# Layer 0 attention as one sequence of 576 steps: value products that lag across groups, output rescaling spread over three engines

## What is computed

```python
qkv = x @ Wqkv                       # x is the normalised, modulated input
q = qkv[..., :2 * Hx].reshape(Bx, 2 * NQ, Sx, HD)      # 32 query heads of 16
k = qkv[..., 2 * Hx:2 * Hx + G].reshape(Bx, NKV, Sx, HD)  # 8 key heads
v = qkv[..., 2 * Hx + G:].reshape(Bx, NKV, Sx, HD)
...
scores = jnp.where(causal, q k^T / sqrt(HD), -inf)
aw = jax.nn.softmax(scores, axis=-1)
aw = aw.reshape(Bx, NQ, 2, Sx, Sx)
aw = aw[:, :, 0] - lam * aw[:, :, 1]
attn = einsum(aw, v) * (1.0 - LAMBDA_INIT)
```

## Time and profile before

| what | us |
|---|---|
| median of three runs (2429.91 to 2431.61) | 2430.19 |
| the profiled execution, its own time | 2430.3 |
| its span | 2428.4 |
| a group in the steady part, from one O3 to the next | 114.88 |
| start of the first step, end of the last output | 129.4, 1947 |

### The profile page before, as it was taken

How to read it: one execution, slowest core, us unless ns; L and a number is a source line. 1 busy time by engine, 2 the same in 40 slices (tenths; PEclk the granted TensorE clock), 3 DMA queues, 4 the chain that set the end, 5 groups by cost and what they waited for, 6 DMA issues and landing times. The chain is left out here.

```text
span 2428.4 us, 46606 instructions
## 1 busy us (share of the span) xinstructions
PE 2220.2 (91%) x17772; PEld 992.5 (41%) x17772; DVE 1829.4 (75%) x3782; ACT 1547.9 (64%) x3105; POOL 525.7 (22%) x584
## 2 busy tenths in 40 slices
PE   6799999999999999999999999999999979889984
PEld 4233333333333333333333333334333258567831
DVE  2788888878787888888888888887888348434467
ACT  2167677777767776767676777777767725235633
POOL 2112121303222121212121213131201014100067
PEclk8589999999999999999999999999999979899955
DMA  4120302121121202020303030212100030000001
GB/s 145 36 58 6 66 11 61 22 50 32 41 41 31 47 25 47 30 56 17 66 6 66 6 66 18 55 27 45 32 12 2 2 96 0 1 1 1 1 22 48
DMA packets 95990, 84.79 MB, mean 35 GB/s; under 512 B 48544, under 2 KB 81440, under 8 KB 95776
## 3 DMA queue, kind: packets, MB, share of 16 engines
q1 hardware_dynamic: 95776, 81.91, 15.2%
HBM read 26.81 MB, written 16.78 MB: 18 GB/s over the span
## 5 line engine op out<-in xcount | busy, mean ns | idle before, releaser
L605 DVE TENSOR_REDUCE m_part<-a_bank 128x1 f32<-128x512 f32 (+3 forms) x2560 | 1395.5, 603 | 270.0 <-PE a_bank L906 163.2
L749 ACT ACTIVATE probs<-b_bank 128x512 f32<-128x512 f32 (+1 forms) x2304 | 1173.2, 578 | 412.4 <-PE b_bank L922 407.2
L922 PE MATMUL b_bank<-q_pack,k_pack 34*128 34x512 bf16 (+7 forms) x5120 | 949.0, 348 | 6.2 <-DMA q_pack<-m_rows 1.8
L894 PE MATMUL a_bank<-k_pack,q_pack 64*128 64x512 bf16 (+3 forms) x2560 | 847.2, 357 | 58.5 <-DVE m_part L605 33.0
L960 PE MATMUL acc<-probs,v_tile 128*32 128x512 f32 (+3 forms) x5120 | 587.1, 540 | 22.6 <-ACT o_sb L756 21.5
L922 PEld LDWEIGHTS b_bank<-q_pack,k_pack 34*128 34x128 bf16 (+1 forms) x5120 | 316.5, 94 | 547.7 <-ACT probs L749 392.6
L894 PEld LDWEIGHTS a_bank<-k_pack,q_pack 64*128 64x128 bf16 x2560 | 238.2, 94 | 333.4 <-DVE m_part L605 255.2
L476 POOL TENSOR_SCALAR_AFFINE_SELECT probs<-probs 128x512 f32<-128x512 f32 (+1 forms) x192 | 151.5, 789 | 1019.4 <-ACT probs L749 1019.4
L906 PE MATMUL a_bank<-future,pick 64*128 64x128 bf16 x2048 | 278.3, 219 | 0.0
L906 PEld LDWEIGHTS a_bank<-future,pick 64*128 64x128 bf16 x2048 | 185.7, 96 | 47.5 <-issue 4.7
L960 PEld LDWEIGHTS acc<-probs,v_tile 128*32 128x32 f32 x5120 | 107.3, 108 | 186.6 <-issue 94.2
(11 more groups left out here) (193 smaller groups left out, 1761.0 us busy)
## 6 DMA issues: line engine op xcount, KB each, us to landing
q_pack<-part SPq DMA_DIRECT2D x384, 64.0 KB, 2.3
k_pack<-part SPq DMA_DIRECT2D x192, 64.0 KB, 2.3
scratch<-qkv_row SPq DMA_DIRECT2D x16, 512.0 KB, 2.8
heads<-scratch SPq DMA_DIRECT2D x16, 512.0 KB, 3.7
xg<-in_L_attn_x SPq DMA_DIRECT2D x16, 256.0 KB, 2.8
scratch<-qkv_row SPq DMA_DIRECT2D x32, 128.0 KB, 2.7
q_pack<-m_rows SPq DMA_DIRECT2D x256, 2.0 KB
x<-in_L_attn_x SPq DMA_DIRECT2D x4, 1024.0 KB, 11.7
```

Source lines behind the costliest of these rows:

```text
L605: dve.tensor_reduce(m_part[:, 2 * hp + side, t, c:c + 1], a_bank[at % A_RING][:, 0:width_a(u % UNITS)], AX.X, ALU.max).then_inc(a_maxed, 1)
L749: act.activation(probs[:, s % P_RING, h, at:C], b_bank[bank_no(("B", par, s, h))][:, at:C], ACT.Exp, scale=HD ** -0.5) \
L894: ins = pe.matmul(a_bank[at % A_RING][:, 0:w], q_pack[buf][rows, hp, 0, q:q + P], k_pack[buf][rows, 0, C * c:C * c + w], start=True, stop= ...
L922: ins = pe.matmul(b_bank[bank_no(slot)][:, at:at + C - q], k_pack[par][rows, n2, P * kt:P * (kt + 1)], q_pack[par][rows, h // 2, n2, C * j ...
```

## The change

The two nested loops over pairs of groups become one loop over `n` from 0 to 578 on every engine.

- The value products of steps 34 and 35 move from the end of their group to steps 0 and 1 of the next one. `meet_v(n - LAG)` crosses groups.
- All uses of a bank (M, O, N, W, T) move from the end of a step to its middle, behind the value product. On ACT they stand between the exponentials of heads 1 and 2. O3 comes at step 2 of the next group. M uses come one step later, T0 to T3 at 18 to 21.
- The copy of `acc` follows the first two exponentials of step `J_LAST + LAG`, and `turn_output` comes one step later.
- Rescaling: ACT copies the turned bank to `o_rows` in SBUF, DVE takes reciprocal and signs from there one step later still (the second after all maxima of that step), and POOL does the multiplication and then the pair.
- `gather_heads` goes from DVE at step 15 to POOL at step 14 for groups 2 to 15.
- The short operations on block maxima are interleaved with the maxima of the next unit; `m_part` is doubled.
- The masks of a short unit stand right behind its scores; where a unit stands alone (`score_maxima`), the two row halves alternate.
- SP issues the same DMAs in the same order with the same waits.

```diff
@@ PE
-                        if s >= LAG:
-                            meet_v(i, par, s - LAG)
-                        two_heads(i, par, s, 1, maxima(1), last)
-                        if ending:
-                            for k in range(LAG):
-                                for u in maxima(2 + k):
-                                    score_maxima(i, par, u)
-                                meet_v(i, par, s - LAG + 1 + k)
-                        for use in [u for t, u in uses_of(par, last) if t == s]:
...
+                if n < LAST_STEP and s in J_FIRST:
+                    pe.wait_ge(m_rows_in, 16 * QH * (NJ * g + J_FIRST.index(s) + 1))
...
+                if n < LAST_STEP:
+                    two_heads(n, 0, share(ahead, 0, 2))
+                if LAG <= n < LAST_STEP + LAG:
+                    meet_v(n - LAG)
+                for use in uses_at(n):
+                    wait_for_bank(use)
...
+                if n < LAST_STEP:
+                    two_heads(n, 1, share(ahead, 1, 2))
+            def score_maxima(u):
+
                 for n in range(2):
-                    unit_head(i, par, u, n)
-                    mask_head(i, par, u, n)
+                    unit_head(u, n)
+                for m in range(2):
+                    for n in range(2):
+                        mask_head(u, n, m)
@@ SP
+            for g in range(GROUPS):
+                par, more = g % 2, g + 2 < GROUPS
+                if more:
+                    load_x(g + 2, g + 2)
+                if g + 1 < GROUPS:
+                    pack(g + 1, 1 - par, STEPS * g)
+                maxima_rows(4 * g + 3, par, 2)
...
@@ ACT
+            for n in range(TAIL):
+                if n < LAST_STEP:
+                    for h in range(QH // 2):
+                        exponential(n, h)
+                if n in COPY_AT:
+                    take_output(COPY_AT[n])
+                for use in uses_at(n):
...
+                    if what == "T" and k % 4 == 3:
+                        first_part(k // 4)
+                if n < LAST_STEP:
+                    for h in range(QH // 2, QH):
+                        exponential(n, h)
+            def take_rows_of_output(block, no, bank):
+                act.wait_ge(misc_filled, no)
+                if block:
+                    act.wait_ge(o_added, block)
+                act.activation(o_rows[:, :], bank[:, :], ACT.Copy).then_inc(o_taken, 1)
@@ DVE
-                dve.reciprocal(o_rl[:, :, :], o[:, :, :, HD]).then_inc(o_step, 1)
-                dve.wait_ge(o_step, upto(2 * n + 1))
-                dve.tensor_tensor(o_w[:, :, :], o_rl[:, :, :], signs[:, :, :], ALU.mult).then_inc(o_step, 1)
...
-                dve.tensor_tensor(o_sc[:, j % 2, :].rearrange("p (t h e) -> p t h e", t=TB, h=QH), o[:, :, :, 0:HD],
+                maximum(u, 0)
+                if before is not None:
+                    negate(before)
+                maximum(u, 1)
+                if before is not None:
+                    negate_rest(before)
...
+                for k, u in enumerate(ahead):
+                    unit_maxima(u, u == UNITS * GROUPS - 1)
+                    if k == 0 and n - 1 in OUTPUT_AT:
+                        invert(OUTPUT_AT[n - 1])
...
+                if n - 1 in OUTPUT_AT:
+                    weigh(OUTPUT_AT[n - 1])
@@ POOL
+                pool.wait_ge(o_weighed, n + 1)
+                if n:
+                    pool.wait_ge(o_added, n)
+                pool.tensor_tensor(o, o_rows[:, :].rearrange("p (t h e) -> p t h e", t=TB, h=QH)[:, :, :, 0:HD],
+                                   o_w[:, :, :].unsqueeze(3).broadcast_to([P, TB, QH, HD]), ALU.mult).then_inc(o_scaled, 1)
+                pool.wait_ge(o_scaled, n + 1)
+                pool.tensor_tensor(dst, halves[:, :, :, 0, :], halves[:, :, :, 1, :], ALU.add).then_inc(o_added, 1)
```

More of the change, by code:

```diff
@@ L137 @@
-GATES_AT = 24
-SLOTS = [slot for par in range(2) for s in range(STEPS)
-         for slot in [("B", par, s, h) for h in range(QH)] + [(use, par, s, 0) for use in MISC[s]]]
-SLOTS[-1:-1] = [None] * (-len(SLOTS) % B_RING)
-def bank_no(slot):
-    return SLOTS.index(slot) % B_RING
-def occupant(slot, last):
-    at = SLOTS.index(slot) - B_RING
-    while True:
-        was = SLOTS[at % len(SLOTS)]
-        if was is not None and (at < 0 or was[0] == "B" or (was[2], was[0]) in uses_of(was[1], last)):
-            return was, at < 0
-        at -= B_RING
+LAST_STEP = STEPS * GROUPS
@@ new lines, with uses_at @@
+NEXT = [j for j in range(NJ) if A_LAST[j] < LEAD]
+PREP_AT = {7: "N", 8: "W0", 9: "W1", 10: "W2", 11: "W3", 18: "T0", 19: "T1", 20: "T2", 21: "T3"}
+COPY_AT = {STEPS * g + J_LAST[j] + LAG: 4 * g + j for g in range(GROUPS) for j in range(NJ)}
+OUTPUT_AT = {n + 1: block for n, block in COPY_AT.items()}
+MAXIMA_AT = {n + 2: 4 * (u // UNITS) + A_LAST.index(u % UNITS)
+             for n in range(LAST_STEP) for u in units(n) if u % UNITS in A_LAST}
+GATHER_AT = 14
+GATES_AT = 24
+def uses_at(n):
+    g, s = n // STEPS, n % STEPS
+    out = []
+    if n in MAXIMA_AT:
+        out.append(("M", MAXIMA_AT[n]))
+    if n in OUTPUT_AT:
+        out.append(("O", OUTPUT_AT[n]))
+    if s in PREP_AT and g + 2 < GROUPS:
+        use = PREP_AT[s]
+        out.append((use[0], g + 2 if use == "N" else 4 * (g + 2) + int(use[1])))
+    return out
@@ L488, in body @@
-            def body(i, last):
-                for par in range(2):
-                    for s in range(STEPS):
-                        if s in DIAG:
-                            mask(i, par, s)
-                        if s == 3 and not last:
-                            inverse_deviation(2 * i + par + 2)
-                        if s in O_AT:
-                            pair(i, par, O_AT[s])
-                        if s == 22 and not last:
-                            split(2 * i + par + 2)
@@ L635, in _ @@
[L635 to L636 removed]
+                unit_maxima(u, False)
             def gates():
@@ new lines, in _ @@
+            for n in range(TAIL):
+                if n < LAST_STEP:
[4 more added lines that the diff above has]
+                for use in uses_at(n):
+                    (what, k), no, bank = use, use_no(use), b_bank[bank_no(use)]
+                    if what == "N":
+                        shift_rows(k, no, bank)
+                    if what == "W":
+                        take_rows(k // 4, k % 4, no, bank)
+                    if what == "T":
+                        take_heads(k // 4, k % 4, no, bank)
+                    if what == "M":
+                        take_maxima(k, no, bank)
+                    if what == "O":
+                        take_rows_of_output(k, no, bank)
+                    if what == "T" and k % 4 == 3:
[3 more added lines that the diff above has]
+                        exponential(n, h)
@@ L926, in score, with two_heads @@
                     ins.then_inc(b_scored, 1)
-            def two_heads(i, par, s, hp, ahead, last):
+            def two_heads(n, hp, ahead):
                 u = ahead[0] if ahead else None
-                score(i, par, s, 2 * hp, 0, last)
+                short = u is not None and width_a(u % UNITS) < C
+                score(n, 2 * hp, 0)
                 if u is not None:
-                    unit_head(i, par, u, 0)
-                score(i, par, s, 2 * hp, 1, last)
+                    unit_head(u, 0)
+                if short:
+                    mask_head(u, 0, 0)
+                    mask_head(u, 0, 1)
+                score(n, 2 * hp, 1)
+                if u is not None and not short:
+                    mask_head(u, 0, 0)
+                    mask_head(u, 0, 1)
+                score(n, 2 * hp + 1, 0)
```

393 lines of the change are left out of this document (164 added, 229 removed).

## The result

| | us |
|---|---|
| after, median of four runs (2472.33 to 2478.16) | 2473.05 |
| before, beside it on the same chip | 2430.05 |
| ratio, 95% interval | 1.0176 [1.0161, 1.0192] |
| profiled execution of after, and its span | 2472.33, 2470.6 |

The change makes the kernel 1.8% slower. The forecast was 2403, with a range that ended at 2440. A group, measured from the value product of one step 0 to the next and averaged over groups 2 to 12, takes 118.37 us, before 114.96. Before, every group takes 114.9 except one at 115.9; after, they vary from 116.2 to 122.5. The 11 steady groups alone bring 37.5 of the 43 us. The last group, from its first score product to the last output, takes 94.3 against 97.5, so the end is not where time is lost.

A forecast was written before the change was run, and what follows sets the result against it. DVE was taken to set the pace in plain steps, PE in steps with a bank use. Groups 1 to 13 gave -16, groups 0, 14, 15 and the lead -4, -2, -4, -1: 2430.2 - 27 = 2403, range 2355 to 2440.

The forecast's parts named there:

- the clock: Rival: waiting 3 us before step 10 brings PE a spell at 1.2 GHz, 1.7 in 14 groups, 2427 us; chance 0.10.
- Part 1: Value products and O3: with the flush gone and acc copied earlier, both PE waits for acc go, -2.1 a group.
- Part 2: SP's queue before step 10: SP starts 3.95 after step 0, a new wait of about 2.9 in groups 1 to 14.
- The rival that the queue isn't late: Rival at step 10: no new wait, steps 0 to 9 take 30.2, -2.9 in 14 groups, 2362 us; chance 0.20.
- Part 3: DVE in steps 10 to 35: less work (scaling, regrouping, output waits) and interleaved short operations, -2.0 a group.
- the pace stays with DVE: Rival in the loop: time taken from PE comes back as waits for the ring, 2430 us; chance 0.10.
- Part 4: ACT and POOL: added work, 2.4 a group on ACT, 0.5 and 2.5 at most on POOL, not on the path.
- Part 5: Bank uses in the middle of a step: -0.4 a group; ACT behind T3 costs +0.6.
- Part 6: Masks: hidden before and after in short units, a little won in single units, -0.2 a group.
- Part 7: DVE's sign product in step 24 waits 0.2 to 4.0 for POOL's split; taken 2.0 against 0.7 before, +1.3.
- The crowding of the last steps: Steps 34 and 35 hold six units without value products to space them; group total 113.3 rounded up to 113.7.
- the slower rival: Rival: DVE locked out for whole POOL operations, sign product 4.0, reciprocal up to 2 more; 2445 us; chance 0.15.

The follow-up runs named there:

- Experiment 11: Kernel of experiment 3 with ACT's copy of acc back behind all four exponentials of the step: 2444.22 us.
- experiment 2: The changed kernel with SP issuing the maxima rows of block 2 ahead of pack instead of behind it: 2444.78 us.
- experiment 3: The changed kernel with both alterations, product with the signs on POOL and maxima rows ahead of pack: 2383.73 us.
- experiment 10: Kernel of experiment 3 with the regrouping of the heads back from POOL at step 14 to DVE at step 15: 2393.18 us.
- experiment 8: Kernel of experiment 7 with only the uses N and W moved back to the end of a step: 2355.23 us.
- experiment 12: Kernel of experiment 3 with the masks in the order they had before the change: 2394.88 us.
- experiment 4: The kernel before the change, with pack waiting for one value product more, the first of the next group: 2509.49 us.
- experiment 7: Kernel of experiment 3 with maxima units spread anew, the planner counting value products of steps 34 and 35 in steps 0 and 1: 2365.54 us.
- experiment 1: The changed kernel with the product of reciprocals and signs made by POOL instead of DVE: 2423.71 us.

## Why the prediction was wrong, point by point

Three terms of its sum failed: the gains in steps 10 to 35, taken at 3.4 a group where 0.6 came; the clock, held at nothing where it cost some 23 us; and the lock-out, for which the middle of two cases was taken. The last one, with the clock behind it, gives the change its wrong sign; the first one is the largest error in us.

- **What bounds the kernel.** Right for the plain step, still 2.50 after.
- **Part 1, the copy and the flush: right.** No wait for `o_sb` is left in after, as forecast, and they were 2.1 a group. Experiment 11 gives 60 us for the copy's place alone, in a kernel where the copy meets the next group's products; in the kernel before it wasn't tried alone.
- **Part 2, the queue: right in place and cause, too dear.** SP was forecast at 3.95 behind step 0 and starts at 725.36 - 721.69 = 3.67; the queue at 27.9 takes 27.3; the rows at 1.2 behind the last issue, 753.72 - 752.64 = 1.08; step 10 at 33.1 comes at 32.0. The wait is 29.4 / 14 = 2.1 a group and not 2.9 (1.6 without group 14), and steps 0 to 9 take 30.6 without it (experiments 2 and 3) and not 30.2. The rival that the queue isn't late, at 0.20, didn't come.
- **Part 3, DVE's work: one piece held, the whole isn't seen.** The regrouping was priced at 0.8 a group and costs 0.7 (experiment 10). But of the 2.0 taken, no wait shows a gain: PE's wait for `m_part` is 23.9 in the kernel before and 24.2 in experiment 3. The rival "the pace stays with DVE" named this.
- **Part 4, ACT and POOL: held.** POOL's copy takes 1.25 us, its scaling 0.62, and PE waits for neither.
- **Part 5, uses in the middle: wrong sign.** Taken at -0.4 a group. Moving N and W back is worth 10 us (experiment 8), so for those the middle costs some 0.7 a group. The +0.6 behind T3 was a little low: 11.1 us in 13 places, 0.85.
- **Part 6, masks: too small.** Taken at -0.2, it is 0.8 a group (experiment 12), by a wait at a short unit that no rival of the prediction named.
- **Part 7, DVE beside the split: the mechanism held, the size failed.** It named the mechanism, the step and both ends, 0.2 and 4.0, and then took the middle, 2.0. The product takes 3.31, and PE loses 3.0. The instruction's start, not a mean over the ends, decides, and the start was wrong by little: "about 7 to 8 us into the split, close to the boundary" at 8.1. It starts 0.8 behind the boundary, and so pays nearly a whole operation. A term whose value jumps from nearly nothing to 4 within 1 us has no middle. Its two ends were two cases. The second half of that rival, a reciprocal that waits too, did not come: 0.24. The Trainium skill (SBUF — State Buffer, Who interferes with whom) sets apart instructions with two SBUF inputs, and the trace agrees on both: 3.31 for the product of two SBUF operands, 0.24 for the reciprocal of one.
- **The clock: held at nothing in the sum.** It was a rival, priced for the queue's wait alone, at a chance of 0.10. It falls behind the lock-out above all, 12 times of 15, loses 32 us in the loop by its record and costs some 23 of time. In experiment 4 it is 27 beyond the wait. The Trainium skill (TensorE: Matmul & The Clock Gate, Why this matters for your kernels) advises against idle gaps between bursts of matmuls; the trace agrees in kind, and its waits of 2.35 are shorter than the gaps that the page speaks of.
- **The crowding of the last steps** was rounded up to 0.4 a group. Spreading the units anew is worth 18 us, 1.3 a group over 14 groups (experiment 7): the planner went on charging the flush to step 35.

**The sum.** The forecast missed by 70 us, and these are its terms. Without its queue term (2.9) and its lock-out term (2.0) the forecast would be 2403 - 14 x 4.9 = 2334; experiment 3, which takes both away, stands at 2384. So **the largest error, 50 us, lies in the gains taken for the rest of the group**. From the first score product of step 10 to the next step 0 the sum takes 84.5 - 2.2 moved out = 82.3 and then -1.4 - 2.0 - 0.4 + 0.6 - 0.2 = -3.4 for parts 1, 3, 5 and 6; experiment 3 has 81.7, so they brought 0.6. A smaller slip adds to it: -2.3 in steps 0 to 9 and -1.4 here are 3.7 of waits that go, while part 1 has 2.1; no source is given for the other 1.6, and 0.81 plus two thirds of 1.3 is 1.7 and not 1.4. Of the 50 us the spread (18), N and W (10) and ACT behind T3 (3 more than taken) are found, and some 19 stay open, and with them why the value products' move into steps 0 to 2 brought no more.

The other 20 are the two losses: 14 x 4.9 = 69 in the forecast, 89 from experiment 3 to after. Here **the clock, a term of nothing in the sum, is the missing one (some 23)**; the lock-out, at 3.0 a group by experiment 1 and 2.7 by experiment 3, was taken some 10 to 14 us too low, and the queue, at 14 x 2.9 = 41 against the 28 of experiment 2, too high by about as much, which hid it. That the slower rival's price and the clock's, added up, give 2445 - 2403 + 2427 - 2403 + 2403 = 2469 and so nearly the 2473 measured is luck: both stand on a base that is 50 too low, and the rival's lock-out was priced above what was measured.

What turned the sign is another matter: with the gains as small as they were, the kernel with the queue's loss alone is at 2424 and with the lock-out's alone at 2445, against 2430 before. The lock-out decides. The rivals weren't exclusive, as the chances had them; they fell on the same kernel.

## What to carry to other kernels

Where the cost of a step depends on when a small instruction meets a long one on another engine, work out both cases, not their middle, and ask what shifts the phase; then move the instruction to the engine that owns the long operations, so that the phase no longer matters. When a value product, or any event that a queue waits for, moves, follow everything behind that wait down to its last consumer: two lines in SP's order were worth 28 us. Mechanisms that fall on the same path are added, and the clock behind them counts as part of each wait's price. A list of small gains in stretches where another engine may set the pace needs a lower bound of its own: here 3.4 a group were taken and 0.6 came.

## What the runs showed of the hardware

- A VectorE operation of 16 columns with two SBUF operands took 3.31 us beside POOL's tensor_tensor and 1.01 us when it started later in one; a reciprocal with one SBUF operand took 0.24 at the same place. In both places it ended within 0.1 us of POOL's operation, in all 14 groups of either kernel alike (3.29 to 3.31, 1.00 to 1.01), which is plainer than in the earlier trace rows.
- Behind a wait of 2.35 us TensorE had a granted clock of 0.66 over 5 us, although it was then busy without a pause. It fell behind 12 of 14 such waits, and in experiment 4 in or behind all 13 waits of 2.9 to 7.2 and not behind one of 1.25. In the kernel before, where PE waits for `acc` for 0.7 at most, all three windows of the group are at 1.00. A stall in front of PE was therefore paid for by more than its length: 78 us for 51 of waiting in experiment 4.
- Between the start of one value product and the next, the same work took 4.14 us at the lowered clock and 2.75 at the full one.
